# Convolution edge stages of a four-layer graph network: links in other steps, products last, GpSimd written out

## What is computed

```
h = silu(edge_scalars @ Wfc1);  w = h @ Wfc2            # 25000 edges, 192 weights each
e0, e1 = (x0 @ Wl1_0)[src], (x1 @ Wl1_1)[src]           # 64 scalars, 32 vectors of 3
mid = w * (e0*sh0, sum(e1*sh1), e0*sh1, e1*sh0)
agg = segment_sum(mid, dst);  conv = agg @ Wl2
x = layernorm(x + selfconnection(x) + alpha * conv)     # 50000 nodes, 160 columns
```

## Time and profile before

| | us |
|---|---|
| median of 3 runs | 4973.63 (4960.56 to 5012.12) |
| profiled execution, its span | 4994.57, 4992.8 |
| setup until the first scaling | 0 to 205.7 |
| edge stages of layers 0, 2, 3 | 205.7 to 864, 2854 to 3516, 3830 to 4485 |
| attention edge stage | about 1325 to 2590 |
| busy PE, DVE, ACT, POOL | 3818.6, 3580.6, 2333.5, 3472.8 |

### The profile page before, as it was taken

The page is one execution under the profiler, slowest core; times in us unless marked ns, Lnnn a source line. Parts: engine busy times, 40 slices in busy tenths (PEclk is TensorE's granted clock), DMA queues, the critical chain, the costliest instruction groups (busy, mean ns, idle before and its releaser), DMA issues. The chain is left out here.

```text
span 4992.8 us, 73391 instructions
## 1 busy us (share of the span) xinstructions
PE 3818.6 (76%) x14102; PEld 1906.0 (38%) x14102; DVE 3580.6 (72%) x8554; ACT 2333.5 (47%) x6704; POOL 3472.8 (70%) x3639
## 2 busy tenths in 40 slices
PE   0399997777599999999950098888897888877675
PEld 0133332555334444444420033333574333335454
DVE  1366665999688888888878645554797555549999
ACT  0133332555555555555536643333797333325555
POOL 1166665999877888878734466676576666759998
PEclk9999998887799999999975599898998999988877
DMA  9322222767555555555549922222896222227665
GB/s 380 96 69 68 66 68 67 223 213 217 159 121 122 124 131 127 125 122 128 128 130 369 311 62 67 66 67 62 273 356 217 68 68 67 68 64 223 190 191 160
DMA packets 593199, 727.86 MB, mean 146 GB/s; under 512 B 80518, under 2 KB 410650, under 8 KB 592980
## 3 DMA queue, kind: packets, MB, share of 16 engines
q1 hardware_dynamic: 499688, 545.80, 36.5%
q0 software_dynamic: 86400, 142.71, 10.9%
q10 hardware_dynamic: 7020, 38.40, 1.8%
HBM read 498.42 MB, written 245.90 MB: 149 GB/s over the span
## 5 line engine op out<-in xcount | busy, mean ns | idle before, releaser
L548 POOL DMA_INDIRECT aggregates<-agg_out,scatter_index x600 | 617.5, 1029 | 410.9 <-issue 252.0
L1294 ACT ACTIVATE y_chunk<-residual,ln_minus_mean_rstd,ln_rstd 128x160 f32<-128x160 f32 x1568 | 700.2, 547 | 371.9 <-POOL ln_minus_mean_rstd L1357 287.5
L1260 PE MATMUL psum<-self_weights,x_chunk_T 128*128 128x160 f32 (+1 forms) x2352 | 491.9, 362 | 64.0 <-ACT x_chunk_T L1307 30.3
L1353 POOL TENSOR_TENSOR ln_rstd<-ln_var_eps,minus_half 128x4 f32<-128x4 f32 x392 | 441.4, 1126 | 142.5 <-DVE ln_var_eps L1442 84.3
L624 PE MATMUL psum<-identity,scaled_x 128*128 128x128 f32 x600 | 145.0, 281 | 498.8 <-ACT scaled_x L570 473.8
L531 POOL DMA_INDIRECT gathered<-x_layer,gather_index x400 | 399.5, 999 | 177.4 <-issue 120.4
L1260 PEld LDWEIGHTS psum<-self_weights,x_chunk_T 128*128 128x128 f32 x2352 | 413.1, 223 | 110.0 <-issue 60.7
L1450 DVE BATCH_NORM_STATS2 ln_stats<-residual 128x6 f32<-128x160 f32 x1568 | 389.4, 307 | 0.1
L531 POOL DMA_INDIRECT gathered<-in_x,gather_index x200 | 208.8, 1044 | 211.2 <-DVE scaled_x L698 123.8
L570 ACT ACTIVATE scaled_x<-gathered,sh_times_attr 128x160 f32<-128x160 f32 x400 | 138.4, 417 | 464.1 <-DVE sh_times_attr L681 308.9
L1338 POOL TENSOR_TENSOR agg_chunk<-agg_chunk,x_chunk 128x640 f32<-128x640 f32 x196 | 327.6, 1671 | 15.4
(11 more groups left out here) (221 smaller groups left out, 10542.4 us busy)
## 6 DMA issues: line engine op xcount, KB each, us to landing
x_layer<-y_chunk SPq DMA_DIRECT2D x294, 320.0 KB, 5.2
x_chunk<-x_layer SPq DMA_DIRECT2D x294, 320.0 KB, 4.7
agg_chunk<-aggregates SPq DMA_DIRECT2D x196, 320.0 KB, 5.4
sh_rows<-in_sh_big SPq DMA_DIRECT2D x50, 768.0 KB
agg_chunk<-aggregates SPq DMA_DIRECT2D x98, 384.0 KB, 6.0
aggregates<-agg_out ACTq DMA_DIRECT2D x48, 768.0 KB
x_chunk<-in_x SPq DMA_DIRECT2D x98, 322.0 KB, 3.1
agg_chunk<-aggregates SPq DMA_DIRECT2D x98, 322.0 KB, 3.8
```

Of the source, the lines that this page charges most:

```text
L548: eng.indirect_dma_start(agg_table[:, :], bass.IndirectOffsetOnAxis(idx_last[:, q, b:b + 1], 0), agg_out[:, q, b, :], None, bounds_check=N ...
L1260: eng.matmul(o[:, b, 0:ns + 96], x_t[:, k4, (2 * half + b) * 128:(2 * half + b) * 128 + 128], self_w[:, k, 0:ns + 96], start=b == 0, stop= ...
L1294: op = eng.activation(y_out[:, buf, b, :], res[:, buf, b, :], ACT.Identity, bias=shift[:, buf, b:b + 1], scale=rstd[:, buf, b:b + 1])
L1353: eng.tensor_tensor(rstd[:, buf, :], var_eps[:, q, :], minus_half[:, 0:T], ALU.pow)\
```

## The change

- Lags in the convolutions become: gather and scaling 0, transposes and F1 1, W1/W2 and E1/E2 and `products` 2, output products and scans 3, transposes back and the copy to `agg_out` 4, scatter 6. On TensorE the output products are a step's last, on ScalarE the scaling is.
- Banks: E1, E2 take TA, TB; W1, W2 take OS, OV2; the transposes back get two banks of their own. `xt1`, `xt2` and `prod` get two buffers.
- F1 gets zero-padded operands of 128 rows and writes `hid` twice (rows 0 to 63, 64 to 127); W1 then works on rows 0 to 63 and W2 on 64 to 127. A1 takes rows 64 to 127 of the products, B1 rows 0 to 63. CN takes 128 rows.
- GpSimd's loop is written out. Its gathers and scatters read their indices in place; the index copies and the waits on them are gone.
- SyncE loads attribute rows and spherical rows in different steps. The setup has 8 more small loads, and VectorE waits for all small loads before it scales the first weight.
- The attention stage's gated vectors overwrite the gates (`vg = gt`); the next gate waits for the last reader.

```diff
-            xt1 = sb("scaled_x_T1", [128, GE], scope=part)
-            hid = sb("hidden", [64, GE], scope=part)
+            xt1 = sb("scaled_x_T1", [128, 2, GE], scope=part)
+            hid = sb("hidden", [128, GE], scope=part)
...
-            prod = sb("products", [128, 2, GE], scope=part)
+            prod = sb("products", [128, 2, 2, GE], scope=part)
...
-            vg = sb("gated_vectors", [96, GE], scope=part)
+            vg = gt
...
+            eng.wait_ge(P["weights_in"], 64)
+            for layer in CONV:
+                fc1, fc2 = BLOCKS.index((layer, "F1")) * 128, BLOCKS.index((layer, "W2")) * 128
+                eng.dma_start(W(layer, "F1")[0:16, 64:128], t["weights"][0:16, fc1:fc1 + 64]).then_inc(P["self_in"], 16)
+                eng.dma_start(W(layer, "W2")[64:128, :], t["weights"][0:64, fc2:fc2 + 128]).then_inc(P["self_in"], 16)
+            for half in (0, 64):
+                eng.dma_start(b1_col[half:half + 64, :], t["small"][0:64, SM["b1"]:SM["b1"] + 2]).then_inc(P["self_in"], 16)
             eng.dma_start(small[:, :], t["small"]).then_inc(P["small_in"], 16)
...
             eng.wait_ge(P["weights_in"], 64)
+            eng.wait_ge(P["self_in"], 16 * (T + 2) * len(SELF) + 128)
             n = 0
...
-            eng.wait_ge(P["self_in"], 16 * (T + 2) * len(SELF))
...
-        TA, TB, H, OS, OV2, OV3, E1, E2 = range(8)
-        W1, W2, R0 = TA, TB, OS
+        TA, TB, H, OS, OV2, OV3, R0, R1 = range(8)
+        W1, W2, E1, E2 = OS, OV2, TA, TB
+        def steps_c(eng, body):
+            steps(eng, NG, body, lead=6, lag=6)
...
+                    eng.dma_start(attr_t[0:K, par, :], t[f"attr{K}"][:, bass.ds(s * GE, GE)])\
+                       .then_inc(S["attr1"] if par else S["attr0"], 16)
+                if live(s, 2, NG):
+                    g = s - 2
+                    apart_from(eng, held(eng, g - 1, S["vec_y"]))
+                    wait(eng, S["vec_y"], g - 1)
+                    eng.dma_start(y_rows[:, par, :], t["sh_big"][96:192, bass.ds(g * GE, GE)])\
+                       .then_inc(S["sh1"] if par else S["sh0"], 16)
+            steps(eng, NG, step, lag=2)
...
-            def step(s, par):
-                held(eng, N - 1)
+            for s in range(NG + 6):
+                par = s % 2
...
-                    eng.tensor_copy(idx_src[:, par, :], src_i[:, bass.ds(g * T, T)]).then_inc(S["index"], 1)
...
+                    wait(eng, S["xs_act"], s - 1)
+                    wait(eng, S["xq"], s - 1)
+                    wait(eng, S["xa"], s - 1)
                     for b in range(T):
+                        col = s * T + b
                         eng.indirect_dma_start(gathered[:, par, b, 0:width], None, x_table[l][:, :],
-                                               bass.IndirectOffsetOnAxis(idx_src[:, par, b:b + 1], 0))\
+                                               bass.IndirectOffsetOnAxis(src_i[:, col:col + 1], 0))\
                            .then_inc(S["gather1"] if par else S["gather0"], 16)
-                if live(s, 3, NG):
-                    g = s - 3
...
+                if live(s, 6, NG):
+                    g = s - 6
-                    eng.tensor_copy(idx_last[:, q, :], last_i[:, bass.ds(g * T, T)]).then_inc(S["index_used"], 1)
...
+                    wait(eng, S["agg"], g + 1)
                     for b in range(T):
-                        eng.indirect_dma_start(agg_table[:, :], bass.IndirectOffsetOnAxis(idx_last[:, q, b:b + 1], 0),
-                                               agg_out[:, q, b, :], None, bounds_check=N - 1, oob_is_err=False)\
-                           .then_inc(sem, 16)
-            steps(eng, NG, step)
+                        col = g * T + b
+                        eng.indirect_dma_start(agg_table[:, :], bass.IndirectOffsetOnAxis(last_i[:, col:col + 1], 0),
+                                               agg_out[:, par, b, :], None, bounds_check=N - 1, oob_is_err=False)\
+                           .then_inc(S["scatter1"] if par else S["scatter0"], 16)
...
-                    wait(eng, S["w_copied"], g)
+                    wait(eng, S["products"], g - 1)
...
+                    eng.matmul(bank(H), W(l, "F1"), attr_t[:, q, :], start=True, stop=True)\
                        .then_inc(S["hidden_mm"], 1)
                 if live(s, 2, NG):
...
+                    wait(eng, S["scan_s"], g - 1)
+                    wait(eng, S["vec_y"], g - 1)
+                    eng.matmul(bank(W1), W(l, "W1")[0:64, :], hid[0:64, :], start=True, stop=True)
+                    eng.matmul(bank(W2), W(l, "W2")[64:128, :], hid[64:128, :], start=True, stop=True)\
+                       .then_inc(S["w_mm"], 1)
+                if live(s, 4, NG):
+                    g = s - 4
                     eng.wait_ge(S["scan_s"], at(S["scan_s"], g + 1))
                     eng.wait_ge(S["scan_v"], at(S["scan_v"], g + 1))
+                    wait(eng, S["agg"], g)
...
+                if live(s, 2, NG):
+                    g = s - 2
+                    eng.wait_ge(S["xt_copied"], at(S["xt_copied"], min(g + 2, NG) if isinstance(g, int) else g + 2))
+                    eng.matmul(bank(E1), W(l, "E1"), xt1[:, par, :], start=True, stop=True)
+                    eng.matmul(bank(E2), W(l, "E2"), xt2[:, par, :], start=True, stop=True).then_inc(S["e_mm"], 1)
+                if live(s, 3, NG):
+                    g, q = s - 3, 1 - par
+                    eng.wait_ge(S["products"], at(S["products"], g + 1))
+                    wait(eng, S["scan_s"], g)
+                    wait(eng, S["w_copied"], min(g + 2, NG) if isinstance(g, int) else g + 2)
+                    eng.matmul(bank(OS, rows_s), W(l, "A1")[64:128, 0:rows_s], prod[64:128, q, 0, :], start=True, stop=False)
+                    eng.matmul(bank(OV2, 96), W(l, "B1")[0:64, 0:96], prod[0:64, q, 0, :], start=True, stop=True)
+                    if l == 0:
+                        eng.matmul(bank(OS, rows_s), W(l, "CN")[:, 0:rows_s], ones_row[:, :], start=False, stop=False)
+                    eng.matmul(bank(OS, rows_s), W(l, "A2")[:, 0:rows_s], prod[:, q, 1, :], start=False, stop=True)
+                    wait(eng, S["vec_m"], g)
+                    eng.matmul(bank(OV3, 96), W(l, "B2")[:, 0:96], prod[:, q, 1, :], start=True, stop=True)\
+                       .then_inc(S["proj"], 1)
+            steps_c(eng, step)
```

More of the change, by code:

```diff
@@ L243, in gnn_kernel @@
                           "rows_in1 scaled scaled1 attr_2 centered centering head_in head_ready head_zeroed self_in self_ready self_zeroed small_in table_zeroed weights_in zeroed")
-        conv_sems = sems("edge", "agg aprod aprod_v attr0 attr1 back e_mm fact gather0 gather1 hidden hidden_mm "
-                                 "index index_used products proj scan_s scan_v scatter0 scatter1 transposed vec_m "
+        conv_sems = sems("edge", "agg aprod aprod_v attr0 attr1 sh0 sh1 back e_mm fact gather0 gather1 hidden hidden_mm "
+                                 "products proj scan_s scan_v scatter0 scatter1 transposed vec_m "
                                  "vec_y w_copied w_mm xa xq xs_act xt_copied ya")
@@ L394, in setup_gpsimd @@
             eng.memset(ones_row[:, :], 1.0).then_inc(P["consts"], 1)
+            eng.memset(attr_t[:, :, :], 0.0).then_inc(P["consts"], 1)
             eng.memset(minus_half[:, :], -0.5).then_inc(P["consts"], 1)
@@ L492, in edge_sync @@
                 stored(eng, l - 1)
+            eng.wait_ge(P["consts"], 4)
             def step(s, par):
                 if live(s, 0, NG):
-                    held(eng, s - 1, S["hidden_mm"])
-                    held(eng, s - 1, S["vec_y"])
-                    apart(eng)
+                    apart_from(eng, held(eng, s - 1, S["hidden_mm"]))
                     wait(eng, S["hidden_mm"], s - 1)
[L500 to L504, removed]
+                    eng.dma_start(attr_t[0:K, par, :], t[f"attr{K}"][:, bass.ds(s * GE, GE)])\
[7 more added lines that the diff above has]
+            steps(eng, NG, step, lag=2)
         def edge_gpsimd(eng, l):
@@ L514, in edge_gpsimd @@
                 eng.wait_ge(P["last"], 1)
-            def step(s, par):
-                held(eng, N - 1)
+            for s in range(NG + 6):
+                par = s % 2
                 if live(s, 0, NG):
[L519 to L523, removed]
-                    eng.tensor_copy(idx_src[:, par, :], src_i[:, bass.ds(g * T, T)]).then_inc(S["index"], 1)
-                    apart(eng)
-                    wait(eng, S["xs_act"], before)
-                    wait(eng, S["xq"], before)
-                    wait(eng, S["xa"], before)
-                    eng.wait_ge(S["index"], at(S["index"], now))
+                    wait(eng, S["xs_act"], s - 1)
+                    wait(eng, S["xq"], s - 1)
+                    wait(eng, S["xa"], s - 1)
@@ L591, in step @@
                     op.then_inc(S["w_copied"], 1)
-                if live(s, 2, NG) and l:
-                    g = s - 2
```

(14 more changed lines are left out.)

141 lines of the change are left out of this document (53 added, 88 removed).

## The result

Changed kernel 5057.39 us (median of 4 runs, 5051.86 to 5062.64), the kernel before beside it 4990.23 (4 runs, 4960.56 to 5012.12): ratio 1.0138, 95% interval 1.0075 to 1.0202. Slower by 1.4%, clear of noise though the interval reaches to both sides of 2%, and outside the range, on the side that I gave 4%. In a later session the same program took **4634.66** (4 runs, 4633.97 to 4643.31) against 4951.77 (13 runs): ratio 0.9368, 0.9343 to 0.9393.

What follows compares the result with a forecast made beforehand. GpSimd's queue was taken to fill 96% of the convolution step. 4994.57 - 318 (edge stages) + 6 (setup) = 4683 us against the profiled execution; against the median 4973.63 - 312 = 4662, range 4590 to 4775.

Steps and rivals of the forecast that it cites:

- the handover: Convolution edge stages: scans, transposes back, E1/E2 and output products in turn take 9.6 us, 10.6 with CN, below GpSimd's step.
- VectorE holds GpSimd up: Rival, 4%: VectorE's denser work delays GpSimd's DMA issues to 1.65 us apart, 13.2 us a step, 5064 us.
- A handover that goes round each step: Rival, 5%: in the convolutions a wait counted as spare recurs each step; 12.0 to 12.6 us stay, about 4960.
- GpSimd's queue: Convolution edge stages: without index copies, GpSimd's eight DMAs set the step at 10.9 us, 11.1 in layer 0.
- the lower bound: GpSimd's step with its eight DMAs at their shortest, 10.1 us; as a case 7%, 4552 us.
- A pair: TensorE, convolutions: two products on different rows start together and cost 1.06 us; W1/W2 took 1.91 before.
- The clock rival: Rival, 14%: TensorE's idle gap halves its clock each step in layers 2 and 3, 12.15 us a step, 4770 us.
- Filling and draining: Ends of each edge stage: 33 us to fill (25 in layer 0), 53 us from last group's gather to landed scatter.
- Setup: Before the edge stages: eight more small loads on SyncE's queue cost +6 us, between 0 and 12.
- The last node stage: Left alone by the change; a node stage moving by over 10 us would mean a missed coupling.
- The sum: Whole kernel: 318 us saved in three edge stages, 6 added in setup; 4683 against the profiled execution, 4662 against the median.

Runs made afterwards that it cites:

- a1: The changed kernel run again, unchanged, in a later session: 4634.66 us, ratio 0.9368 to the kernel before.
- e9: Changed kernel, GpSimd still written out, with two index copies a step, their waits, and DMAs reading the copied indices: 4944.29 us, ratio 0.9989; on another chip 4944.25.
- e11: Changed kernel with two index copies a step and their waits, but DMAs read indices in place, so copies are idle: 4942.23 us, ratio 0.9977.
- e14: Changed kernel with two idle, awaited index copies a step and no waits for landed DMAs: 4938.26 us, ratio 0.9961; on another chip 4950.28.
- e12: Changed kernel with GpSimd's old loop, each copy bringing two steps' indices, so one copy a step: 4831.16 us, ratio 0.9756; on another chip 4837.72.
- e7: Changed kernel with GpSimd's old loop, index copies and waits back, new lags kept: 4940.90 us, ratio 0.9964.
- e13: Changed kernel with GpSimd's old loop and copies of every step, and both pairs of products taken apart: 4960.55 us, ratio 1.0026.
- e1: Changed kernel with both pairs taken apart (W1/W2 and A1/B1 one behind the other): 5139.87 us, ratio 1.0356.
- e2: Changed kernel with only the pair W1/W2 taken apart, A1/B1 kept: 5104.09 us, ratio 1.0295.
- e3: Changed kernel with only the pair A1/B1 taken apart, W1/W2 kept: 5091.30 us, ratio 1.0262.
- e15: Changed kernel with two GpSimd waits added for the landing of its own DMAs of two steps ago, no copies: 4709.26 us, ratio 0.9514.
- e5: Changed kernel with a small GpSimd memset behind every four DMAs, awaited by GpSimd: 5015.18 us, ratio 1.0134.

## Why the prediction was wrong

**The failed step is the handover** ("With five lags, what still has to follow in turn is ... Sum 9.6 us", and the waits "that set nothing"). It takes for granted that an engine goes on as soon as the instruction before it has ended. In the first comparison rises were 12 us late and more, and what follows in turn took over 13 us a step in place of 9.6, above GpSimd's 10.9. The 129 steps came out 2.7 us longer on average than forecast, 344 us; drains (65 to 68 us for 53) and the filling (42 to 43 for 33) took some 60 more. The last node stage, 47 us shorter, gave some back. What makes the rises late stays open.

The trace of before had a sign of it, which I overlooked. None of its rises is late in the convolution stages, but its attention stage, whose GpSimd program is written out and reads its indices in place already, has 43 rises over 1 us late, up to 3.8, and waits for "remote" (us in all, times, longest):

```profile
ACT message_scalars L920 <- remote: 42.9, 12, 3.8
```

Two rivals touch the result. By its number the nearest is "VectorE holds GpSimd up" (5064, 4%), and that is luck: it wanted DMAs 1.5 us and more apart, and they were 1021 and 1034 ns long with 0.30 between. A handover that goes round each step (4960, 5%) has the right sign in GpSimd's profile: it waits for the scaling. It had the wrong mechanism and was 97 us short.

The other steps can be read in a1, where rises are on time.

*GpSimd's queue* was right, and its size near the lower bound. The timeline of GpSimd in a1, one step:

```profile
3902.69 0.99 POOL L537 DMA_INDIRECT gathered<-x_layer,src_index  x1 [0.31 <-issue]
3903.99 0.98 POOL L537 DMA_INDIRECT gathered<-x_layer,src_index  x1 [0.30 <-issue]
3905.28 0.95 POOL L537 DMA_INDIRECT gathered<-x_layer,src_index  x1 [0.30 <-issue]
3906.53 1.62 POOL L537 DMA_INDIRECT gathered<-x_layer,src_index  x1 [0.30 <-issue]
3908.46 1.02 POOL L547 DMA_INDIRECT aggregates<-agg_out,last_index  x1 [0.30 <-issue]
3909.78 1.00 POOL L547 DMA_INDIRECT aggregates<-agg_out,last_index  x1 [0.31 <-issue]
3911.08 0.98 POOL L547 DMA_INDIRECT aggregates<-agg_out,last_index  x1 [0.30 <-issue]
3912.37 0.98 POOL L547 DMA_INDIRECT aggregates<-agg_out,last_index  x1 [0.30 <-issue]
3913.66 0.99 POOL L537 DMA_INDIRECT gathered<-x_layer,src_index  x1 [0.31 <-issue]
```

Eight DMAs without a gap, 1.25 to 1.32 apart, one of them longer: 10.97 us. The means are 10.61 and 10.76 for 10.9, and 10.41 in layer 0 for 11.1, since its gathers came down to 963 ns from the 1044 of the earlier trace rows. Two copies a step make 12.4 to 12.8 (e9, e11, e14), one 11.65 to 11.90 (e12), none 10.41 to 10.76, so a copy costs 0.8 to 1.0 us in layers 2 and 3 and more in layer 0. The new order and pairs with the copies left in (e7, ratio 0.9964) gain next to nothing: the queue is what had to go.

*TensorE.* The timeline of PE in a1:

```profile
3900.52 0.64 PE L661 MATMUL psum<-products,weights 64*65 64x512 f32 x1
3900.53 0.67 PE L662 MATMUL psum<-products,weights 64*96 64x512 f32 x1
...
3901.55 1.07 PE L665 MATMUL psum<-products,weights 128*65 128x512 f32 x2
3902.46 1.02 PE L667 MATMUL psum<-products,weights 128*96 128x512 f32 x2
3905.86 0.33 PE L625 MATMUL psum<-identity,scaled_x 128*128 128x128 f32 x1 [2.38 <-ACT scaled_x L603]
...
3906.79 1.78 PE L630 MATMUL psum<-edge_attr_rows,weights 128*128 128x512 f32 x2
```

A pair takes 1.03 us (forecast 1.06), and the idle time lies in one piece ahead of the transposes with the scaling as its releaser, as forecast. Under GpSimd's copies the pairs are worth 16 to 20 us (e13 against e9 beside it, which is written out, and against e7 on another chip). The clock rival, a fall in each step, didn't come, as the windows of a1 show (0.99 and 0.97; 0.88 and 0.87 in the first comparison, where TensorE stood idle more):

```profile
205.00:755.00 550.00, 463.07 (x1800) 192.76 (x1800) 393.76 (x803) 198.81 (x452) 387.72 (x391) 0.99 0.28 78
3662.00:4166.00 504.00, 407.48 (x1602) 165.55 (x1598) 305.09 (x422) 219.35 (x557) 376.10 (x368) 0.97 0.27 78
```

But it came in some steps, the one shown among them: the granted clock was 1.2 GHz from 3906.92 to 3910.33, 1.1 us behind the end of the idle 2.38, and F1 (L630) took 1.78 us in place of 1.02. In layer 3's stage of a1 there are 9 such stretches in 50 groups, in the kernel before 22. The Trainium skill ("TensorE: Matmul & The Clock Gate", Part 4) says that a transpose doesn't count as TensorE being busy in the same way; the step shown, with transposes behind the gap and a fall, agrees with it, and most steps kept the full clock. Nor did VectorE hold GpSimd up: but for single longer ones the issues are 1.25 to 1.32 us apart.

*Filling and draining* were 35 to 39 us for 33 (layers 2 and 3) and 56 to 65 for 53. Layer 2's stage took 557.9 and layer 3's 549.1, for 555. Setup: the first transposes start at 214.6 in place of 207.5, 7 us later (forecast 6).

*The last node stage* moved, against the forecast: 461 us behind the last scatter of layer 3 for 507. This was so in the first comparison too (460), and in e1, e2 and e3; in every other run it takes 507 to 513. It goes with GpSimd's small products there, first in a1, then in e15, whose program differs by two waits in other stages and whose last stage takes 509:

```profile
L1359 POOL TENSOR_TENSOR ln_rstd<-ln_var_eps,minus_half 128x4 f32<-128x4 f32 x97 | 99.4, 1024 | 0.1
```

```profile
L1361 POOL TENSOR_TENSOR ln_rstd<-ln_var_eps,minus_half 128x4 f32<-128x4 f32 x97 | 142.6, 1470 | 0.1
```

What sets the one or the other stays open.

*The sum.* Between the traces of before and a1 lie 361 us: 319 in the three edge stages with the setup, where I had forecast 312, and 46 in the last node stage, where I had forecast nothing, less 5 in between. So the sum was right part by part where it had a part. Against the traced execution it gave 4683, and a1 is 48 us under that, nearly all of it the node stage. Against 4662, where I had taken off 21 us because the median lay under the traced execution, it is 27 us under. Against the median of before in its own session a1 gains 317 us, and since before was not traced there, where the two medians of before differ isn't known.

## What to carry to other kernels

A plan by queues and durations supposes that a semaphore rises when its instruction ends. Look for waits released by "remote", in every stage, also in one that the change leaves alone: they tell that it didn't, and no engine's busy time will. Taking the last slack out of one engine's stream of DMAs can cost more than it gains in one session and give its full worth in another, so a change of this kind wants timing in more than one session and on more than one chip before it is judged.

## What was not expected of the hardware

TensorE's rises 12 us late and more, with VectorE's and ScalarE's on time, in the first three sessions, and never in the last three. The recordings of the two kinds differ as well: in the first comparison some 2148 of TensorE's 2390 rises are recorded and 40417 by DMAs, in a1 all and 63924. Rises are missing in the kernel before too (some 2119 and 47735) and in e7, where none is late, so a gap in the recording doesn't make a rise late by itself. The late sessions came first, and each session whose chip is on record had its own, so chip, time and the recording itself, which every run here carried, aren't told apart. What GpSimd's copies (e7) have that awaited memsets (e5) don't stays open as well: e9, e14 and e15 would tell it, run where rises are late.
